# Flamingo layer on one core: each engine's repeated turn is replaced by one straight list over all eight batches

## The chip, the cores and the metric

One core of a Trainium2 chip runs the whole program. The metric is the device time of one execution in microseconds (us). The core has five engines that run side by side, each through its own instructions in order: TensorE (PE in the profile; PEld are its weight loads), VectorE (DVE), ScalarE (ACT), GpSimd (POOL) and SyncE (SP, which issues the DMAs). They wait for each other through semaphores.

## What is computed

For eight batches of 512 tokens with 256 features:

```python
emb  = layernorm(x) + ctx
q, k, v = emb @ wq + bq, emb @ wk + bk, emb @ wv + bv
ew   = exp(w - max(w));  w = pos_bias inside a band of 64, else 0
num  = ew @ (exp(k - max_k) * v);  den = ew @ exp(k - max_k)
attn = (sigmoid(q) * num / den) @ wo + bo
n1   = norm(attn + emb) * gamma + beta
n2   = norm(relu(n1 @ w1 + b1) @ w2 + b2 + n1) * gamma + beta
x1   = x + tanh(g_xattn) * n2
xq   = act_quant(layernorm(x1))
gate, up = silu(xq @ weight_quant(w_gate).T), xq @ weight_quant(w_up).T
out  = x1 + tanh(g_ffn) * (act_quant(gate * up) @ weight_quant(w_down).T)
```

`weight_quant` rounds a whole matrix to three values, by the mean of its magnitudes; `act_quant` rounds each token to 8 bits, by its maximum.

## The kernel before

A batch is four tiles of 128 tokens. Its work is cut into pieces, each a small function of one engine, named by batch `b` and a tile or half. In the order of the data they are:

- x and ctx come by `fetch_x`, `fetch_ctx` (SP, one buffer each). The first norm: `tile_stats(b, 0, t)` and `mean_variance` (DVE), `rsqrt(b, 0)` (POOL), `normalise(b, 0)` (ACT), `embed` (POOL) adds ctx. `emb_rows` transposes on PE; `emb_upper` (ACT) and `emb_lower` (DVE) split the result into a high and a low part, and this pair of splits follows every transposition of the float part: a product of two split operands is three matmuls (`product`, L1258 to L1267, so that all of them show as L1265).
- `keys_T`, then `key_max`, `max_bias` (DVE), `max_row` (PE) and `bias_parts` (DVE) give the row that `keys_values` (PE) adds to keys and values. `queries` and `half_sigmoid` (ACT) make the gate of attention. Per tile, `exp_keys`, `copy_values` (ACT), `weighted` (DVE), `e_upper` (ACT) and `e_lower` (DVE) make the pair e, ev.
- `attend(b, "num" or "den", half, j)` multiplies tile j's near weights; `key_sums`, `sum_upper`, `sum_lower` and `attend_far` add what lies outside the band. `inverse` (DVE reciprocal), `gated`, `divided`, `y_upper`, `y_lower`, `project` (PE), `first_residual` (DVE, on top of `add_bo` of POOL), norm 1 (`normalise_tile`), `n1_rows`, `n1_upper`, `n1_lower`.
- Feed-forward: eight of `hidden` (PE), `hidden_upper`, `hidden_whole` (ACT), `hidden_lower` (DVE), `feed_forward` (PE); `second_residual` (DVE), norm 2, `n2_gamma`, `first_sum` (POOL) give x1.
- The bit part: norm 3, `token_max`, `token_scales` (DVE), `token_quantise` (ACT), `xq_rows`, `xq_columns`; per tile `gate`, `up` (PE), `silu` (ACT), `product`, `product_scale` (DVE), `quantise` (POOL for even tiles, ACT for odd), `hq_rows` (PE), `hq_columns` (ACT), `down` (PE), `output` (DVE). `store` after four outputs.

Nearly all tiles in SBUF are single: x_in, emb, the pair e, n1T, a2, x1, out_t; h has four places. PSUM has eight banks for everything; `BANK_USES` gives each piece one bank (gate and up: two neighbours), the same for every batch, and `bank_wait` makes PE wait for the bank's last reader.

The order is written out: each engine has one function `turn(n, b0, ..., b4)`, with its pieces in a fixed order, where b2, b3, b4 are the batches n-2, n-3, n-4. `turns` calls it for n = 0 to 4 and 8 to 11 as straight code, and for n = 5, 6, 7 in a loop (`Fori`), in which the semaphore values are worked out from the loop's register. In a turn, b2 goes from the first norm to e and to `attend(b2, "num", 0 and 1, 0)`; b3 has the rest of attention, projection, norm 1, feed-forward, norms 2 and 3 up to `product(b3, 1)`; b4 has the rest of the bit part. The preparation of weights (`masks`, `position_max`, `exp_positions`, `positions_T`, `ewT_upper`; the splits; `sum_of_magnitudes`, `bit_scale`, `bit_round`, `bit_clip`, `bit_rows`, `bit_columns` for the three quantised matrices; `beta_w1` for b1) stands in the turns 0 to 3 under `if n == ...`.

## Time and profile before

| | us |
|---|---|
| median of 3 runs | 746.5 (746.36 to 746.93) |
| the profiled execution | 753.5 |
| its span, first to last instruction | 751.7 |
| busy in it: PE, DVE, ACT, POOL | 544.9, 439.7, 381.4, 213.7 |
| mean granted clock of TensorE, of full speed | 0.933 |
| moved between HBM and core | 25.12 MB |

The profile is of one execution. Its page lists busy times by engine, then the chain of work that ended last (followed back from the last instruction, at each step to what released it), then the costliest groups of instructions. Windows give each engine's busy time in a stretch; a timeline lists instructions by start. "x" is a count of instructions; L and a number is the line in the kernel, which can be that of a helper; in square brackets stands the idle time of an engine before an instruction, and what ended it. A clock of 1.00 is the higher of the two levels of TensorE (2.4 GHz), the lower is 1.2 GHz.

### The profile page before, as it was taken

The page shows a single profiled execution, that of the slowest core. Times are in us where ns is not written, and L with a number is a line of the kernel's source. Part 1 is how long each engine was busy: PE and PEld are TensorE (multiplying, and loading weights), DVE is VectorE, ACT ScalarE, POOL GpSimd, SP SyncE. Part 2 cuts the span into 40 slices and gives each one's busy share as a digit, 9 for nine tenths or more (in the row PEclk, how much of TensorE's full clock was granted, in tenths as well). Part 3 has the DMA queues.
Part 4 walks back from the last instruction along what each step waited for, and adds up shares of the span by engine and source line. Part 5 has one row for each costly group of instructions (what it writes and reads, how often), then busy time and mean ns, then how long its engine had stood idle before and what let it go on. Part 6 is the DMA issues. An engine that isn't in the chain of part 4 may idle for free.

```text
span 751.7 us, 10043 instructions
## 1 busy us (share of the span) xinstructions
PE 544.9 (72%) x3248; PEld 440.3 (59%) x3270; DVE 439.7 (58%) x907; ACT 381.4 (51%) x589; POOL 213.7 (28%) x232
## 2 busy tenths in 40 slices
PE   0539578587986779677968698777968697769534
PEld 0537567464865567555956486556846595547413
DVE  2254724568465954587366855596457836694236
ACT  0665145444646356644654565635664464545334
POOL 2330016301361026301640136102730155013211
PEclk9999879789998999899998999899989999899859
DMA  7540000200002000300030000200030001000000
GB/s 237 160 146 17 1 1 0 84 1 1 1 29 84 1 1 2 112 0 0 0 104 7 0 0 16 95 0 2 0 113 1 0 2 56 1 1 1 28 1 28
DMA packets 25208, 25.12 MB, mean 33 GB/s; under 512 B 3154, under 2 KB 24148, under 8 KB 25172
## 3 DMA queue, kind: packets, MB, share of 16 engines
q1 hardware_dynamic: 24336, 24.65, 10.0%
q8 instruction: 21, 0.34, 0.2%
q10 hardware_dynamic: 836, 0.01, 0.1%
q14 instruction: 15, 0.12, 0.1%
HBM read 20.46 MB, written 4.19 MB: 33 GB/s over the span
## 4 chain that ended last, share of the span: by engine, by line
PE 43%; DVE 29%; issue 10%; ACT 9%; POOL 4%; DMA 2%; SPq 1%; DVEq 0%; ACTq 0%; POOLq 0%
PE ps L1265 35%; DVE ps L976 5%; DVE st L920 4%; DVE cols L1049 2%; DVE work L1043 2%; POOL rstd L407 2%; DVE bias_row L953 2%; ACT work L587 2%; ACT work L593 2%; PE ps L1397 1%; ACT work L682 1%; DVE cols L1024 1%; DVE e_lo L967 1%; DVE work L1000 1%; DVE n1T_lo L1005 1%
## 5 line engine op out<-in xcount | busy, mean ns | idle before, releaser
L404 POOL TENSOR_TENSOR mv<-mv,cols 128x4 f32<-128x4 f32 x32 | 6.5, 204 | 326.2 <-DVE mv L928 326.2
L1011 DVE TENSOR_TENSOR h_lo<-ps,h_hi 128x512 fp32r<-128x512 f32 x64 | 43.5, 690 | 89.5 <-ACT ps L658 89.5
L653 ACT ACTIVATE h_hi<-ps,cols 128x512 fp32r<-128x512 f32 x64 | 44.1, 690 | 60.8 <-PE ps L1265 48.7
L682 ACT ACTIVATE work<-ps,cols 128x1024 f32<-128x1024 f32 x32 | 35.7, 1114 | 72.5 <-PE ps L1397 56.6
L1265 PE MATMUL ps<-w_hi,h_hi 128*128 128x256 f32 x256 | 72.2, 282 | 0.0
L1265 PE MATMUL ps<-w_lo,h_hi 128*128 128x256 f32 x256 | 72.1, 282 | 0.0
L1265 PE MATMUL ps<-w_hi,h_lo 128*128 128x256 f32 x256 | 71.9, 281 | 0.0
L1265 PE MATMUL ps<-ew_hi,e_hi 128*128 128x256 f32 x128 | 42.6, 333 | 37.5 <-DVE e_lo L967 37.5
L1043 DVE TENSOR_TENSOR work<-work,ps 128x1024 f32<-128x1024 f32 x32 | 38.8, 1213 | 41.6 <-ACT work L682 41.4
L1265 PE MATMUL ps<-n1T_hi,w_hi 128*128 128x512 f32 x128 | 52.2, 408 | 10.3 <-DVE n1T_lo L1005 10.3
L694 ACT ACTIVATE hqT<-ps,cols 128x1024 bf16<-128x1024 f16 x32 | 35.6, 1112 | 40.7 <-PE ps L1416 40.7
L976 DVE RECIPROCAL ps<-ps 128x512 f32<-128x512 f32 x16 | 53.8, 3359 | 0.8 <-PE ps L1342 0.6
L1424 PE MATMUL ps<-wdT,hqT 128*128 128x256 bf16 x256 | 33.2, 272 | 27.5 <-DVE work L1067 16.9
L1265 PEld LDWEIGHTS ps<-ew_hi,e_hi 128*128 128x128 f32 x128 | 28.7, 224 | 41.2 <-DVE e_lo L967 40.9
L1265 PE MATMUL ps<-n1T_lo,w_hi 128*128 128x512 f32 x128 | 51.4, 402 | 0.0
L1265 PE MATMUL ps<-n1T_hi,w_lo 128*128 128x512 f32 x128 | 51.2, 400 | 0.0
L1265 PEld LDWEIGHTS ps<-w_lo,h_hi 128*128 128x128 f32 x256 | 48.2, 188 | 1.4
L1265 PEld LDWEIGHTS ps<-w_hi,h_hi 128*128 128x128 f32 x256 | 48.0, 187 | 1.4
L1265 PEld LDWEIGHTS ps<-w_hi,h_lo 128*128 128x128 f32 x256 | 48.4, 189 | 0.0
L1424 PEld LDWEIGHTS ps<-wdT,hqT 128*128 128x128 bf16 x256 | 23.1, 97 | 36.2 <-issue 26.0
L587 ACT ACTIVATE work<-work,nmr,rstd 128x256 f32<-128x256 f32 x64 | 33.2, 589 | 21.8 <-POOL nmr L410 21.7
L1397 PE MATMUL ps<-wuT,xqT 128*128 128x512 bf16 x121 | 31.3, 391 | 14.0 <-DVE work L982 13.6
(180 smaller groups left out, 1561.4 us busy)
## 6 DMA issues: line engine op xcount, KB each, us to landing
x_in<-in_x_dram SPq DMA_DIRECT2D x8, 512.0 KB, 4.7
emb<-in_ctx_dram SPq DMA_DIRECT2D x8, 512.0 KB, 5.9
work<-in_x_dram SPq DMA_DIRECT2D x8, 512.0 KB, 3.7
out_dram<-work SPq DMA_DIRECT2D x8, 512.0 KB, 3.0
work<-in_L_xattn_w_dram SPq DMA_DIRECT2D x2, 1024.0 KB, 8.8
place_c<-in_L_xattn_pos_bias_dram SPq DMA_DIRECT2D x1, 1024.0 KB, 9.3
work<-in_L_ffn_w_gate_dram SPq DMA_DIRECT2D x1, 1024.0 KB, 5.5
work<-in_L_ffn_w_up_dram SPq DMA_DIRECT2D x1, 1024.0 KB, 5.7
```

The source lines that it names most:

```text
L407: pool.tensor_tensor(rstd[:, n, :], mv[:, n, :, 1], minus_half, ALU.pow).then_inc(rstd_ok[n].sem, 1)
L587: last = nc.scalar.activation(dst[:, t, :], src[:, t, :], ACT.Identity, bias=nmr[:, n, t:t + 1], scale=rstd[:, n, t:t + 1])
L653: nc.scalar.activation(h_hi[:, m % RING, :], bank("h", m), ACT.Relu, bias=b1_col[:, m:m + 1]).then_inc(h_hi_ok.sem, 1)
L682: nc.scalar.activation(sg, bank_pair("gate", t), ACT.Silu, scale=sgate[:, t:t + 1]).then_inc(sg_ok.sem, 1)
L694: nc.scalar.activation(hqT[:], bank_h("hqT", t).rearrange("p (k n) -> p k n", n=P), ACT.Identity, bias=unlift_col, scale=LIFT_SCALE).then_ ...
L920: nc.vector.bn_stats(st6[:, n, t, :], src[:, t, :]).then_inc(stats[n].sem, 1)
L976: nc.vector.reciprocal(bank("den", h), bank("den", h)).then_inc(rden_ok.sem, 1)
L1011: nc.vector.tensor_tensor(h_lo[:, m % RING, :], bank("h", m), h_hi[:, m % RING, :], ALU.subtract).then_inc(h_lo_ok.sem, 1)
L1043: nc.vector.tensor_tensor(prod[t % 2].rearrange("p (a n) -> p a n", a=2), sg.rearrange("p (a n) -> p a n", a=2), bank_pair("up", t), ALU.m ...
L1265: last = nc.tensor.matmul(dst, lhsT, rhs, start=(i == 0 and not begun), stop=(i == n - 1 and ends))
L1397: last = nc.tensor.matmul(dst[:, c, :], xqT[:, k, t * P:(t + 1) * P], w[:, k, c * T:(c + 1) * T], start=(k == 0), stop=(k == ND - 1))
L1424: last = nc.tensor.matmul(bank("down", t)[:, 0:D], hqT[:, k, :], wdT[:, k, :], start=(k == 0), stop=(k == NH - 1))
```

## The change

`turn`, `turns` and the loop are gone on all five engines. Each engine runs a straight list of pieces with constant batch numbers (536 on PE, 582 on DVE, 464 on ACT, 107 on POOL), in another order than the turns had. The pieces issue the same instructions as before. `BANK_USES` becomes `BANK`, with a bank for each piece and each batch; `bank_wait` follows the list and waits for the last reader of that bank; the banks used once for weights (`EWT_BANKS`, `TOTAL_BANKS`, `BIT_BANKS`, `B1_BANK`) are tracked the same way. On POOL some waits for vectors move from `rows` into the pieces that need them. The core of the diff:

```diff
-BANK_USES = (
-    ("xqT", 0, 4, 1, 1), ("gate", 0, 4, 0, 2), ("up", 0, 4, 6, 2), ("up", 1, 4, 2, 2), ("gate", 1, 4, 0, 2),
...
+BANK = {
+    ("embT", 0): (0, 5, 1, 5, 4, 0, 2, 6), ("embT", 1): (1, 4, 6, 7, 2, 6, 4, 0), ("kT", 0): (4, 4, 1, 0, 4, 0, 2, 6),
+    ("kT", 1): (5, 5, 6, 7, 0, 2, 6, 0), ("mx", 0): (0, 3, 1, 6, 1, 3, 7, 4), ("kv", 0): (0, 1, 7, 7, 4, 0, 2, 4),
+    ("kv", 1): (1, 3, 6, 6, 6, 4, 0, 0), ("kv", 2): (2, 6, 1, 2, 5, 1, 3, 1), ("kv", 3): (3, 4, 6, 3, 7, 5, 1, 2),
...
+    ("den", 1): (0, 2, 0, 1, 3, 7, 5, 5), ("o", 0): (0, 0, 7, 4, 0, 2, 1, 1), ("o", 1): (6, 6, 6, 5, 1, 3, 5, 2),
...
+    ("gate", 3): (0, 2, 6, 4, 4, 2, 6, 0), ("up", 3): (2, 6, 4, 0, 2, 6, 0, 4), ("hqT", 3): (7, 4, 0, 2, 5, 0, 4, 6),
...
+        held = {}
 
         def bank_wait(b, step, n=0):
...
+            first = BANK[step, n][b]
+            c, per = last_reader[step]
+            for place in range(first, first + (2 if step in PAIRED else 1)):
+                for s, k in held.get(place, ()):
+                    nc.tensor.wait_ge(s, k)
+                held[place] = ((c.sem, c.at(b, (n + 1) * per)),)
```

SP's list (`x_again` is the second load of x, for x1):

```diff
-                if b2 is not None:
-                    fetch_x_again(b2)
-                if n == 2:
-                    fetch_gate()
-
-            turns(sp, turn)
+            fetch_positions()
+            fetch_w2()
+            fetch_x_again(0)
+            fetch_ctx(0)
+            fetch_x(0)
+            fetch_wqo()
+            fetch_gate()
+            fetch_w1()
+            fetch_x(1)
+            fetch_wkv()
+            fetch_vectors()
+            fetch_ctx(1)
+            fetch_up()
+            fetch_down()
+            fetch_x(2)
+            fetch_ctx(2)
+            fetch_x(3)
+            fetch_x_again(1)
+            fetch_ctx(3)
+            fetch_x(4)
+            store(0)
+            fetch_x_again(2)
+            fetch_ctx(4)
+            fetch_x(5)
+            store(1)
+            fetch_x_again(3)
+            fetch_ctx(5)
+            fetch_x(6)
+            store(2)
+            fetch_x_again(4)
+            fetch_ctx(6)
+            fetch_x(7)
+            store(3)
+            fetch_x_again(5)
+            fetch_ctx(7)
+            store(4)
+            fetch_x_again(6)
+            store(5)
+            fetch_x_again(7)
+            store(6)
...
```

PE's list: its head, one cycle of the steady part, and the end.

```diff
+            positions_T()
+            emb_rows(0, 0)
+            emb_rows(0, 1)
+            total(0)
+            queries(0, 0)
+            queries(0, 1)
+            bit_rows(0)
+            keys_T(0, 0)
+            keys_T(0, 1)
+            max_row(0)
+            beta_w1()
+            keys_values(0, 0)
+            keys_values(0, 1)
+            keys_values(0, 2)
+            keys_values(0, 3)
+            attend(0, "num", 0, 0)
+            attend(0, "den", 1, 0)
+            attend(0, "den", 1, 1)
+            attend(0, "den", 0, 0)
+            attend(0, "den", 0, 1)
+            emb_rows(1, 0)
...
+            project(3, 0)
+            project(3, 1)
+            project(3, 2)
+            project(3, 3)
+            keys_values(4, 0)
+            keys_values(4, 1)
+            keys_values(4, 2)
+            keys_values(4, 3)
+            hq_rows(1, 3)
+            attend(4, "num", 0, 0)
+            attend(4, "den", 1, 0)
+            attend(4, "den", 1, 1)
+            attend(4, "den", 0, 0)
+            attend(4, "den", 0, 1)
+            down(1, 3)
+            attend(4, "den", 1, 2)
+            attend(4, "den", 0, 2)
+            attend(4, "num", 1, 0)
+            attend(4, "num", 0, 1)
+            key_sums(4)
+            n1_rows(3, 0)
+            attend(4, "den", 1, 3)
+            n1_rows(3, 1)
+            attend(4, "num", 0, 2)
+            attend(4, "num", 0, 3)
+            attend_far(4, "num", 0)
+            attend(4, "den", 0, 3)
+            attend_far(4, "den", 0)
+            attend_far(4, "den", 1)
+            attend(4, "num", 1, 1)
+            hidden(3, 0)
+            attend(4, "num", 1, 2)
+            attend(4, "num", 1, 3)
+            attend_far(4, "num", 1)
+            hidden(3, 1)
+            hidden(3, 2)
+            feed_forward(3, 0)
+            feed_forward(3, 1)
+            xq_rows(2)
+            hidden(3, 3)
+            hidden(3, 4)
+            hidden(3, 5)
+            hidden(3, 6)
+            feed_forward(3, 2)
+            gate(2, 0)
+            up(2, 0)
+            emb_rows(5, 0)
+            feed_forward(3, 3)
+            feed_forward(3, 4)
+            gate(2, 1)
+            gate(2, 2)
+            hidden(3, 7)
+            up(2, 1)
+            hq_rows(2, 0)
+            feed_forward(3, 5)
+            up(2, 2)
+            down(2, 0)
+            up(2, 3)
+            emb_rows(5, 1)
+            feed_forward(3, 6)
+            keys_T(5, 0)
+            keys_T(5, 1)
+            hq_rows(2, 1)
+            feed_forward(3, 7)
+            hq_rows(2, 2)
+            down(2, 1)
+            queries(5, 0)
+            down(2, 2)
+            max_row(5)
+            queries(5, 1)
+            gate(2, 3)
+            project(4, 0)
+            project(4, 1)
+            project(4, 2)
+            project(4, 3)
+            keys_values(5, 0)
+            keys_values(5, 1)
+            keys_values(5, 2)
+            keys_values(5, 3)
...
+            feed_forward(7, 6)
+            xq_rows(6)
+            feed_forward(7, 7)
+            gate(6, 0)
+            up(6, 0)
+            gate(6, 1)
+            gate(6, 2)
+            up(6, 1)
+            up(6, 2)
+            up(6, 3)
+            hq_rows(6, 0)
+            gate(6, 3)
+            down(6, 0)
+            hq_rows(6, 1)
+            down(6, 1)
+            hq_rows(6, 2)
+            down(6, 2)
+            hq_rows(6, 3)
+            down(6, 3)
+            xq_rows(7)
+            gate(7, 0)
...
```

DVE's list over a part of the head, and a part of a cycle:

```diff
+            emb_lower(0, 0)
+            emb_lower(0, 1)
+            bit_scale(0)
+            tile_stats(1, 0, 0)
+            tile_stats(1, 0, 1)
+            tile_stats(1, 0, 2)
+            bit_clip(0)
+            tile_stats(1, 0, 3)
+            mean_variance(1, 0)
+            wkv_lower()
+            key_max(0, 0)
+            key_max(0, 1)
+            max_bias(0)
+            bias_parts(0)
+            b1_whole()
+            w1_lower()
+            weighted(0, 0)
...
+            tile_stats(2, 0, 2)
+            tile_stats(2, 0, 3)
+            bit_clip(1)
+            gated(0, 0)
+            bit_clip(2)
+            gated(0, 1)
+            inverse(0, 0)
+            weighted(1, 0)
+            divided(0, 0)
+            inverse(0, 1)
...
+            bias_parts(4)
+            first_residual(3, 0)
+            tile_stats(3, 1, 0)
+            tile_stats(3, 1, 1)
+            product(1, 3)
+            first_residual(3, 1)
+            product_scale(1, 3)
+            weighted(4, 0)
+            tile_stats(3, 1, 2)
+            tile_stats(3, 1, 3)
+            weighted(4, 1)
+            mean_variance(3, 1)
+            e_lower(4, 0)
+            weighted(4, 2)
+            e_lower(4, 1)
+            e_lower(4, 2)
+            weighted(4, 3)
+            output(1, 3)
+            e_lower(4, 3)
+            tile_stats(2, 3, 0)
+            tile_stats(2, 3, 1)
+            tile_stats(2, 3, 2)
+            tile_stats(2, 3, 3)
+            sum_lower(4)
+            mean_variance(2, 3)
+            n1_lower(3, 0)
+            n1_lower(3, 1)
+            inverse(4, 0)
...
```

POOL's list over one cycle, and the start of ACT's:

```diff
+            rsqrt(3, 1)
+            first_sum(2)
+            n1_gamma(3)
+            rsqrt(2, 3)
+            add_b2(3)
+            x_beta(3)
+            add_bo(4)
+            embed(5)
+            quantise(2, 0)
+            rsqrt(6, 0)
+            quantise(2, 2)
...
+            w2_upper()
+            exp_positions()
+            ewT_upper(0)
+            ewT_upper(1)
+            ewT_upper(2)
+            ewT_upper(3)
+            wo_upper()
+            wq_upper()
+            normalise(0, 0)
+            sum_of_magnitudes(0)
+            emb_upper(0, 0)
+            emb_upper(0, 1)
+            bit_round(0)
+            wkv_upper()
+            bit_columns(0)
+            normalise(1, 0)
+            w1_upper()
+            gates_and_bias()
+            half_sigmoid(0, 0)
+            half_sigmoid(0, 1)
+            exp_keys(0, 0)
...
```

## Rows read from the trace of the kernel before

**Rows 1.** The page: busy time, ended-last chain by engine, three groups (busy, mean ns | idle before)
```profile
PE 544.9 (72%) x3248; PEld 440.3 (59%) x3270; DVE 439.7 (58%) x907; ACT 381.4 (51%) x589; POOL 213.7 (28%) x232
...
PE 43%; DVE 29%; issue 10%; ACT 9%; POOL 4%; DMA 2%; SPq 1%; DVEq 0%; ACTq 0%; POOLq 0%
...
L1011 DVE TENSOR_TENSOR h_lo<-ps,h_hi 128x512 fp32r<-128x512 f32 x64 | 43.5, 690 | 89.5 <-ACT ps L658 89.5
...
L1043 DVE TENSOR_TENSOR work<-work,ps 128x1024 f32<-128x1024 f32 x32 | 38.8, 1213 | 41.6 <-ACT work L682 41.4
...
L976 DVE RECIPROCAL ps<-ps 128x512 f32<-128x512 f32 x16 | 53.8, 3359 | 0.8 <-PE ps L1342 0.6
```

**Rows 2.** Windows: start:end, length, busy PE, PEld, DVE, ACT, POOL, clock, DMA share, GB/s
```profile
52.00:100.42 48.42, 34.65 (x181) 29.22 (x181) 25.91 (x44) 20.39 (x32) 3.72 (x5) 0.87 0.07 23
270.34:352.37 82.03, 64.27 (x394) 51.80 (x397) 52.41 (x109) 44.38 (x70) 25.21 (x27) 0.96 0.08 26
352.37:434.20 81.83, 64.34 (x393) 51.83 (x397) 52.39 (x109) 44.36 (x70) 25.15 (x27) 0.96 0.08 26
598.58:680.05 81.47, 63.97 (x393) 51.67 (x397) 52.25 (x108) 44.53 (x70) 28.68 (x29) 0.96 0.04 14
703.00:751.70 48.70, 18.14 (x127) 10.33 (x126) 21.52 (x55) 19.46 (x24) 10.28 (x14) 0.77 0.06 22
```

**Rows 3.** Windows inside one turn, columns as above
```profile
352.37:375.30 22.93, 22.93 (x146) 20.77 (x147) 8.89 (x22) 13.83 (x22) 11.34 (x9) 1.00 0.00 0
392.30:397.60 5.30, 0.03 (x1) 0.00 (x0) 3.05 (x8) 5.05 (x11) 0.00 (x0) 0.78 0.47 154
397.60:413.00 15.40, 14.96 (x82) 11.87 (x85) 9.83 (x17) 6.32 (x8) 1.29 (x2) 0.86 0.00 0
```

**Rows 4.** The chain that ended last, inside the same turn: start, length, what
```profile
382.84 2.22 DVE bias_row L953
...
394.48 1.23 DVE cols L1024
```

**Rows 5.** Timeline of PE: start, length, instruction; at the low and the high clock
```profile
398.20 0.41 PE L1265 MATMUL ps<-ew_hi,e_lo 128*128 128x256 f32 x1
398.41 0.41 PE L1265 MATMUL ps<-ew_hi,e_hi 128*128 128x256 f32 x1
...
439.56 0.28 PE L1265 MATMUL ps<-w_hi,h_hi 128*128 128x256 f32 x1
439.67 0.28 PE L1265 MATMUL ps<-w_lo,h_hi 128*128 128x256 f32 x1
...
439.91 0.39 PE L1265 MATMUL ps<-n1T_hi,w_hi 128*128 128x512 f32 x1
440.14 0.39 PE L1265 MATMUL ps<-n1T_lo,w_hi 128*128 128x512 f32 x1
```

**Rows 6.** Timeline of the head, all engines: start, length, instruction, idle before
```profile
9.51 0.28 DVE L831 CAST bias_row<-bkv_row 1x256 fp32r<-1x256 f32 x1 [6.75 <-DMA bkv_row<-in_L_xattn_bv_dram]
...
12.21 1.93 POOL L378 TENSOR_SCALAR_AFFINE_SELECT place_c<-place_c 128x2048 f32<-128x2048 f32 x1 [10.64 <-DMA place_c<-in_L_xattn_pos_bias_dram]
...
20.83 1.91 ACT L540 ACTIVATE w_hi<-work 128x2048 fp32r<-128x2048 f32 x1 [15.80 <-DMA work<-in_L_xattn_w_dram]
...
28.77 6.83 PE L1237 MATMUL ps<-cols,work 128*128 128x1 f32 x32
...
51.91 1.94 PE L1273 MATMUL ps<-ident,emb 128*128 128x128 f32 x8
...
61.33 0.47 PE L1310 MATMUL ps<-bias_row,ones_r 128*128 128x512 f32 x1
```

**Rows 7.** Timeline of the tail, columns as above
```profile
712.53 2.34 POOL L449 TENSOR_TENSOR work<-work 128x1024 f32<-128x1024 f32 x1
...
726.99 0.14 PEld L1397 LDWEIGHTS ps<-wgT,xqT 128*128 128x128 bf16 x2 [1.64 <-issue]
...
747.87 0.48 DVE L1067 SCALAR_TENSOR_TENSOR work<-ps,cols,work 128x256 f32<-128x256 f32 x1 [2.47 <-PE ps L1424]
```

2162 lines of the change are left out of this document (1607 added, 555 removed), and 5 rows, old and new, of the table BANK.

## The prediction

> **What bounds the kernel now.** I read the page first. The matrix engine (PE) is the busiest at 544.9 us, yet that is 72% of the span, and the chain that ended last is only 43% PE [rows 1]: no engine is full, so order and latency set the time. The windows cut at each batch's first `hidden` matmul show the rhythm: every batch costs 81.5 to 82.0 us, of which PE is busy 64, DVE 52, ACT 44, POOL 25 to 29 [rows 2]. The windows inside one turn show where PE's missing 17.5 us are. In the feed-forward stretch PE is full (22.93 of 22.93); behind keys_values it stands still for 5.3 us, and then runs a stretch at a mean granted clock of 0.86, part of it at 1.2 GHz [rows 3]. The chain says why: behind keys_values of batch b2 the third norm of b3 is worked off (ACT normalises, DVE takes the token maximum at 394.48), and only then comes e_lower(b2, 0), for which `attend` waits [rows 4]; later two reciprocals of 3.36 [rows 1] and the first norm stand between attention and feed-forward of the same batch. So one turn is 22.93 us of feed-forward plus a 59 us chain in which PE has 41.4 us of work. A turn holds attention, projection, norm and feed-forward of **one** batch (b3), which makes that chain unavoidable in it.
>
> **The change, part by part.**
>
> *No loop.* Nine of twelve turns were written out before; three (n = 5 to 7) ran in the loop. The batches whose period lies within the loop took 82.0 and 81.8 us, and one wholly written out 81.5 [rows 2]. So writing out is worth 0 to 0.5 us for each of three turns; I take 0. The Trainium skill (Runtime: NRT & Kernel Launch, Instruction fetch mechanics) says that a taken branch breaks the sequential prefetch and forces a stall, while a long straight program streams; by it something would be gained per pass. By those rows it is under 0.5 us, and I add nothing.
>
> *PSUM banks per batch, semaphores on constants.* No added instruction; each bank waits for its last reader only. Price 0, above zero only where a chosen bank ties two stages: in the list for batch 4, `o` of batch 3 lies in banks 4 and 5, which kv 0 and kv 2 of batch 4 take, and `up(…, 3)` in banks 6 and 7, which kv 1 and kv 3 take. These readers stand just before in DVE's list; I count 1.5 us of PE idleness per cycle for them.
>
> *The new order.* In the steady part, between two feed-forwards of batch f, PE now has project(f+1), keys_values(f+2), nearly all of attend(f+2), key_sums(f+2) and n1_rows(f+1). The first norm of f+1 runs under kv and attend of f+2; reciprocals of f+2 run under hidden(f); gate, up and down of f-1 are spread through the feed-forward of f. What follows what across the waits:
> - PE's own work. Two 512-column matmuls start 0.23 us apart, two 256-column ones at the high clock 0.12, as 48 of the one and 96 of the other make 22.93 us; at the low clock 0.21 [rows 3, 5]. Counted out by these, a batch is 61 us; the 64.3 of [rows 2] less the excess of the 15 attend matmuls and 8 transposes run slowly (about 2 us) gives 62. I take 62.
> - Entry to kv: bias_parts must be done. Its cast took 2.22 us [rows 4] where the same cast elsewhere took 0.28 [rows 6]; with the rest it is 1.2 to 3.1 us after max_row, and PE has queries(…, 1), gate(…, 3) and four projects, 5.2 us, in between. Covered at either price. The Trainium skill (SBUF — State Buffer, SBUF: two separate sides) has a reason: a cast in a two-port mode and a GpSimd instruction lock each other out; POOL has no large operation at that place of the new lists. By the rule the cast falls back to 0.28, by the old row it stays; the sum is the same.
> - kv to attend: DVE has ahead of e_lower(…, 0) two residual additions (0.69 each, as h_lo), product(…, 3) (1.21 [rows 1]), its maximum (1.23, as the token maximum [rows 4]) and some fifteen instructions of 0.1 to 0.45: about 8 us, against 7.2 us of kv and hq_rows on PE plus the bank waits above; then e_lower(…, 3) about 5 us later against 4.1 us of attends. Idle: 1 + 1 us.
> - Feed-forward stretch: with gate, up and down in it, PE has 35 us of work and DVE about 33 busy (two reciprocals of 3.36 [rows 1], eight h_lo, three products with maxima), 35 with its gaps. They are level, so I allow 1 us.
> - POOL: the sums end about 2 us before emb_rows needs them. Free, with little cover; if they come late, all of the lateness is paid in each cycle.
>
> Together 62 + 4.5 = **66.5 us per batch** where it was 81.9.
>
> *The head.* Before, positions landed as about the second MB (masks at 12.2), w2 as the fifth (20.8), and emb_rows(0) began at 51.9 [rows 6]: some 0.24 MB/us. Now positions are first, then w2, x and ctx of batch 0: they land at about 7, 11 and 16.5. Masks to 11, maximum, w2_upper, exponentials to 16, transposes and ewT to 21, two weight copies, normalise(0, 0) to 24, embed to 26.5: emb_rows(0) at 27. But SP holds wkv behind fetch_x(1), which waits for that embed: wkv lands at 33; keys_T(0) at 34.5; then beta_w1 (6.8 us, [rows 6]) waits for the vectors, which are queued behind wkv, and keys_values(0) starts near 45, where it was 61.3 [rows 6]. w_up waits for beta_w1 and w1_lower, w_down behind it lands near 58; its rounding and clips stand in ACT's and DVE's lists ahead of batch 0's division. So the last attend_far(0) comes at 66, project(0) at 80, and hidden(0, 0) at **93** (100.4 before), but with attention of batch 1 already done.
>
> *Between.* hidden(0) to hidden(1) has no gate work and no cover for batch 1's norms: 24 us of feed-forward, 9.5 to kv(2), 15 of kv, attend and n1: **49**. Then five cycles at 66.5 (1 to 6): **332.5**. From hidden(6) to hidden(7) there is no new batch: 43 us of PE work and some idleness: **47**. Feed-forward of 7: **24**.
>
> *The tail.* Before, 48.7 us follow the last feed-forward [rows 2]; gate and down of batch 6 were long under way. The new list leaves all of gate(6) to down(6) behind feed_forward(7, 7), and first_sum(7) waits for the fourth output of 6. One batch from its first gate weights to its last output took 726.99 to 748.35, so 21.4 us; from first_sum to the end of the span it was 712.53 to 751.7, so 39.2 [rows 7]. With batch 7's second norm mixed in: 21.4 + 39.2 + 1.4 = **62**, 13 us more than now.
>
> *Sum.* 93 + 49 + 332.5 + 47 + 24 + 62 = 607.5 us of span. The profiled execution took 753.5 us (span 751.7, 1.8 around it), 7.0 above the median of 746.5; so 607.5 + 1.8 - 7.0 = **602.3 us**.
>
> **The rivals.**
> - *DVE becomes the bound.* For: 52.4 us busy [rows 2], an in-order list of 109 instructions, level with PE in the longest stretch. Against: 14 us of slack per cycle. It decides where DVE's waits per cycle exceed those; at 20 us of waits the period is 73: 5 x 6.5 = 32 more, 635.
> - *PE is filled.* For: the waits that I counted are each about 1 us and the cast is cheaper. Period 62.5: 20 less, 582.
> - *The chain stays.* The change doesn't do what it says: single buffers (x_in, emb, e, n1T, a2, x1) or a bank tie batch f+1 to f as before and the period stays 82: 602 + 5 x 15.5 = 680. Against: the longest ring that I find, output(f) to store to ctx to embed to quantise(f+1) to output(f+1), is some 40 us.
> - *Slower: SP's queue as a convoy.* store(b) stands before x_again(b+2) and ctx(b+3); if every load waits out the whole bit part of an old batch, stages run in series. To reach 746 the period must be (751.7 - 275) / 5 = 95 us, so the ring of 40 would need to be over twice as long. It is not in the rows.
>
> **How the numbers follow.** Forecast (590 to 620) 0.58; DVE-bound (620 to 650) 0.20; PE filled (575 to 590) 0.13; chain stays (650 to 744) 0.07; slower 0.02. The range 580 to 640 leaves out the two last and the outer ends of the second and third. A measurement of this kernel tells 0.2% (1.5 us) from no change; within that lies nearly nothing: 0.01. Faster 0.97, slower 0.02.
>
> **What would show it.** In the profile after: hidden of neighbouring batches 66.5 us apart in the middle and PE busy about 62 of it at a granted clock near 1.0; no gap of 5 us before the first attend; the cast of bias_parts at 0.3 us; emb_rows(0) near 27, hidden(0, 0) near 93; 62 us after the last feed-forward. I am wrong if the gaps before e_lower or product(…, 0) are several us, if beta_w1 or w_down come late, or if the head's waits push hidden(0, 0) past 100.

## The result and the profile after

The changed kernel takes **591.4 us** (median of 4 runs, 589.24 to 592.88); the kernel before took 746.7 us beside it. The ratio is 0.790 (95% interval 0.786 to 0.795). The forecast was 602.3 us, range 580 to 640: the direction is right, the time lies inside the range, and the forecast was 10.9 us too high.

The profiled execution took 589.24 us, its span 587.5. Its page, with the lines that answer to [rows 1] (busy time, share, instructions; then groups with busy time, mean ns | idle before them and its releaser):

```profile
PE 509.9 (87%) x3270; PEld 416.9 (71%) x3270; DVE 438.4 (75%) x907; ACT 373.3 (64%) x587; POOL 216.5 (37%) x232
...
L1436 DVE TENSOR_TENSOR h_lo<-ps,h_hi 128x512 fp32r<-128x512 f32 x64 | 42.9, 680 | 19.2 <-ACT ps L741 19.1
...
L1401 DVE RECIPROCAL ps<-ps 128x512 f32<-128x512 f32 x16 | 53.7, 3354 | 1.2 <-PE ps L2220 1.2
L1468 DVE TENSOR_TENSOR work<-work,ps 128x1024 f32<-128x1024 f32 x32 | 38.7, 1211 | 20.6 <-ACT work L765 17.6
```

The work is nearly the same: DVE was busy for 438.4 us (before 439.7), and a reciprocal still takes 3354 ns. ACT loads its table 12 times instead of 14, 1.3 us each. What went is idleness: DVE stood 19.2 us in front of h_lo where it had stood 89.5, and PE is busy 87% of the span instead of 72%.

The windows of after, cut as in [rows 2] at each batch's first `hidden` matmul (start:end, length, then busy PE, PEld, DVE, ACT, POOL, granted clock, DMA share, GB/s): the head, hidden(0) to hidden(1), 1 to 2, two steady cycles, and what follows the last feed-forward:

```profile
0.00:98.72 98.72, 62.83 (x366) 54.22 (x367) 64.99 (x128) 54.71 (x86) 32.38 (x38) 0.90 0.37 112
98.72:141.48 42.76, 42.52 (x262) 37.49 (x263) 31.91 (x72) 24.92 (x48) 19.45 (x21) 1.00 0.12 38
141.48:208.43 66.95, 64.74 (x421) 53.34 (x420) 54.03 (x111) 44.25 (x71) 25.66 (x28) 1.00 0.10 32
208.43:271.07 62.64, 61.04 (x397) 50.05 (x397) 51.85 (x109) 43.72 (x70) 25.35 (x27) 1.00 0.11 35
271.07:333.70 62.63, 61.03 (x397) 50.04 (x397) 51.84 (x109) 43.72 (x70) 25.40 (x27) 1.00 0.11 35
...
525.00:587.50 62.50, 31.57 (x200) 16.95 (x198) 34.25 (x81) 29.11 (x33) 12.86 (x18) 0.78 0.05 18
```

A batch costs 62.64 us instead of 81.9. Of these 19.3 us, 16.0 are PE idleness (17.6 before, 1.6 now) and 3.3 are PE's own busy time (64.3 to 61.03): the granted clock of a cycle rose from 0.96 [rows 2] to 1.00, and the stretch at 0.86 behind the gap of 5.3 us [rows 3] is gone with the gap.

| stretch | forecast | measured | difference |
|---|---|---|---|
| start to hidden(0, 0) | 93 | 98.7 | +5.7 |
| hidden 0 to 1 | 49 | 42.8 | -6.2 |
| hidden 1 to 6, five cycles | 332.5 | 314.6 | -17.9 |
| hidden 6 to 7 | 47 | 45.3 | -1.7 |
| feed-forward of 7 | 24 | 23.6 | -0.4 |
| from there to the end | 62 | 62.5 | +0.5 |
| span | 607.5 | 587.5 | -20.0 |
| from span to median | -5.2 | +3.9 | +9.1 |
| median | 602.3 | 591.4 | -10.9 |

Where PE stood in the kernel before, over three cycles (270.34 to 515.85 us; line, releaser: us in total, times, longest):

```profile
PE ps L1265 <- DVE e_lo L967: 15.9, 3, 5.4
PE ps L1424 <- DVE work L1067: 7.4, 3, 2.5
PE ps L1397 <- DVE work L982: 5.8, 3, 1.9
PE ps L1265 <- DVE n1T_lo L1005: 5.1, 4, 1.3
PE ps L1265 <- DVE work L982: 4.2, 3, 1.4
...
PE ps L1359 <- ACT work L593: 0.3, 2, 0.2
```

The idleness was spread over about a dozen places. The largest is the 5.3 us in front of `attend`, which waits for `e_lower`. In front of `n1_rows` (L1359), where the first norm must be done, PE stood only 0.2 us: `up`, `down` and `hq_rows` of the older batch lay ahead of it, with 2.5 us of waiting in front of that `down` (L1424). 1.3 us more followed in front of `hidden` (n1T_lo). The 1.4 us in front of `queries` and the 1.9 us in front of `up` are waits for a bank: PE waits until `gated` (L982) has read the bank that it is to write.

Two things said ahead of the result were wrong. The pieces don't all issue the same instructions as before: in `bias_parts` the diff turns `nc.vector.tensor_copy(bias_row[0:1, 0:D], mrow)` into `nc.vector.tensor_tensor(bias_row[0:1, 0:D], mrow, mrow, ALU.max)`, one instruction per batch, which I had overlooked. And the lists have 576 pieces on PE, 586 on DVE and 468 on ACT, where 536, 582 and 464 were given.

### The profile page after: what moved, and what is told of

The parts are those of the page before. It is cut to its first block and busy times, and to the rows that moved or that the text cites. A ratio compares the mean times of both kernels' runs of the same rounds, so it can differ in the third digit from the quotient of the medians.

```text
span 587.5 us, 9784 instructions
## 1 busy us (share of the span) xinstructions
PE 509.9 (87%) x3270; PEld 416.9 (71%) x3270; DVE 438.4 (75%) x907; ACT 373.3 (64%) x587; POOL 216.5 (37%) x232
## 5 line engine op out<-in xcount | busy, mean ns | idle before, releaser
L2143 PE MATMUL ps<-w_hi,h_hi 128*128 128x256 f32 x256 | 75.2, 294 | 5.3 <-DVE h_lo L1436 5.3
L1436 DVE TENSOR_TENSOR h_lo<-ps,h_hi 128x512 fp32r<-128x512 f32 x64 | 42.9, 680 | 19.2 <-ACT ps L741 19.1
L1401 DVE RECIPROCAL ps<-ps 128x512 f32<-128x512 f32 x16 | 53.7, 3354 | 1.2 <-PE ps L2220 1.2
L1468 DVE TENSOR_TENSOR work<-work,ps 128x1024 f32<-128x1024 f32 x32 | 38.7, 1211 | 20.6 <-ACT work L765 17.6
L461 POOL TENSOR_TENSOR cols<-cols 1x1 f32<-1x1 f32 x16 | 2.9, 183 | 130.8 <-DVE cols L1483 130.7
L1345 DVE BATCH_NORM_STATS2 st<-work 128x6 f32<-128x256 f32 x96 | 34.9, 413 | 12.0 <-POOL work L456 11.5
L741 ACT ACTIVATE ps<-ps,cols 128x512 f32<-128x512 f32 x64 | 41.7, 652 | 0.0
L1474 DVE TENSOR_REDUCE cols<-work 128x1 f32<-128x1024 f32 x32 | 38.8, 1211 | 0.4
```

Of the source, the lines that this page charges most:

```text
L741: nc.scalar.activation(bank(b, "h", m), bank(b, "h", m), ACT.Relu, bias=b1_col[:, m:m + 1]).then_inc(h_relu_ok.sem, 1)
L1345: nc.vector.bn_stats(st6[:, n, t, :], src[:, t, :]).then_inc(stats[n].sem, 1)
L1401: nc.vector.reciprocal(bank(b, "den", h), bank(b, "den", h)).then_inc(rden_ok.sem, 1)
L1436: nc.vector.tensor_tensor(h_lo[:, m % RING, :], bank(b, "h", m), h_hi[:, m % RING, :], ALU.subtract).then_inc(h_lo_ok.sem, 1)
L1468: nc.vector.tensor_tensor(prod[t % 2].rearrange("p (a n) -> p a n", a=2), sg.rearrange("p (a n) -> p a n", a=2), bank_pair(b, "up", t), AL ...
L1474: nc.vector.tensor_reduce(hm[:, t:t + 1], prod[t % 2], AX.X, ALU.max, apply_absolute_value=True).then_inc(hm_ok.sem, 1)
```

## The experiments

Medians of device time; ratios are to the kernel before, timed on the same chip, with 95% intervals. Periods are the distances between neighbouring hidden(b, 0) in the profiled execution.

### Is it the loop?

This is the kernel before with its three looped turns written out:

```diff
-            for n in range(TURNS):
-                whole(n)
-            with eng.Fori(TURNS, NB) as n:
-                turn(None, *[n - age for age in range(TURNS)])
-            for n in range(NB, NB + TURNS - 1):
+            for n in range(NB + TURNS - 1):
                 whole(n)
```

> The kernel before with its loop written out: the same turns in the same order, twelve times straight code, all waits on constants. Theory (the order brought the gain, the loop cost nothing): 746.5 us, within 1.5 of it, since batches inside and outside the loop had the same period (82.0, 81.8 and 81.5 us). Rival (giving up the loop is itself worth something: branches, semaphore values from registers): up to 0.5 us per turn by the rows, more if a stall hides elsewhere: 740 or less.

Measured: 747.23 us (10 runs), ratio 1.0015 [0.9976, 1.0053]. The batches whose period lies in the former loop take 81.4 to 82.4 us, as the others. Giving up the loop was worth nothing that can be measured, so the gain is that of order and banks together; no run separates these two. The Trainium skill (Runtime: NRT & Kernel Launch, Instruction fetch mechanics) says that a taken branch whose target has not been fetched stalls the engine; over these three turns no such stall shows.

### What is the changed instruction worth?

The instruction was changed once alone in the kernel before, and once undone in the changed kernel:

```diff
-                nc.vector.tensor_copy(bias_row[0:1, 0:D], mrow).then_inc(bias_hi_ok.sem, 1)
+                nc.vector.tensor_tensor(bias_row[0:1, 0:D], mrow, mrow, ALU.max).then_inc(bias_hi_ok.sem, 1)
```

> The kernel before with one instruction changed, the one that the diff also changed in bias_parts: tensor_copy(bias_row, mrow) becomes tensor_tensor(mrow, mrow, max). In the turns the copy takes 2.2 us and lies on the chain that ended last; it ends just as POOL's n2_gamma ends. If only the copy's mode makes it wait for POOL, the new form takes 0.4 us there too and each of seven turns is up to 1.8 us shorter: 746.5 - 12 = 734 us. If an instruction with two inputs in SBUF waits for POOL as well (as the Trainium skill says, SBUF — State Buffer, SBUF: two separate sides), nothing changes: 746.5 us, and the 0.41 us of the kernel after come from POOL standing idle at that place of its list.

> The kernel after with the old tensor_copy put back in bias_parts, everything else as it is. Theory (bias_parts is covered by queries, gate and four projects on PE in the new order): 591.4 us, within 2, whether the copy takes 0.3 or 2.3 us. Rival (the replaced copy was a real part of the gain): 1.9 us for each of seven batches, 604 us.

Measured: 748.18 us, ratio 1.0025 [0.9991, 1.0058], and 594.25 us, ratio 0.796 [0.791, 0.801]. The instruction itself, by line (duration ns min/median/max; first and last start), in the kernel before, in before with the maximum, in the changed kernel and in that with the copy:

```profile
L953 DVE CAST bias_row<-bkv_row x8: 280/2206/2222, 60.5 to 628.9; 1x256 fp32r<-1x256 f32 x8
```

```profile
L953 DVE TENSOR_TENSOR bias_row<-bkv_row x8: 413/2345/2351, 58.8 to 622.1; 1x256 fp32r<-1x256 f32 x8
```

```profile
L1378 DVE TENSOR_TENSOR bias_row<-bkv_row x8: 411/411/414, 45.4 to 439.9; 1x256 fp32r<-1x256 f32 x8
```

```profile
L1378 DVE CAST bias_row<-bkv_row x8: 280/282/282, 45.6 to 443.1; 1x256 fp32r<-1x256 f32 x8
```

In the old place both forms take over 2.2 us (medians); in the new one they take 0.28 and 0.41. The place decides, not the form; my theory of a gain in the old kernel fell. In the lists the copy gives periods of 62.66, so it is covered, as the prediction had it. The medians of the two lists differ by 2.8 us, and by 1.7 us against the changed kernel run again (592.53, below). In the profiled executions the kernel with the copy was 1.5 us longer between hidden(1) and hidden(2) and 1.6 us longer after the last feed-forward than the changed kernel. In the first of these stretches PE's waits are the same and the granted clock is 0.98 against 1.00, and the instruction itself is shorter (0.28 against 0.41); so nothing points at the instruction.

### Is it the cover of the first norm?

The kernel is the changed one, but for batches 3 to 5 `n1_rows(b, ·)` stands right behind `project(b, 3)` on PE, ahead of kv and attend of batch b+1; on ACT and DVE the pieces that feed it are moved forward with it. The core of the diff, for b = 3:

```diff
             normalise_tile(3, 0)
...
+            n1_lower(3, 0)
+            n1_lower(3, 1)
...
+            n1_rows(3, 0)
+            n1_rows(3, 1)
...
-            n1_rows(3, 0)
...
-            n1_rows(3, 1)
```

> The kernel after, where for batches 3, 4 and 5 the first norm is no longer covered: on PE n1_rows(b) stands right behind project(b, 3) and before keys_values(b+1), and DVE's and ACT's parts of that norm are moved ahead of the e parts of b+1 to match. Same instructions, same PE work. Theory (the gain is the cover of such chains by the next batch's work): residual, statistics, rsqrt, four normalise and n1_rows show on PE as 7 to 9 us of idleness in each of three cycles: 591.4 + 24 = 615 us. Rival (the gain is a better filling in general, and other work closes such a gap): under 3 us per cycle, below 600 us.

Measured: 626.22 us, ratio 0.839 [0.833, 0.844]; the three periods are 71.6, 73.8 and 75.0 us: 9.0, 11.1 and 12.4 more. What PE waited for in 208 to 435 us (line, releaser: us in total, times, longest), and one of these cycles in the columns of the windows:

```profile
PE ps L2237 <- ACT work L676: 21.7, 3, 7.4
PE ps L2143 <- DVE h_lo L1436: 4.9, 3, 1.8
```

```profile
283.85:357.62 73.77, 63.45 (x395) 52.36 (x397) 52.98 (x109) 44.03 (x70) 25.30 (x28) 0.93 0.09 30
```

PE stands 7.2 us in front of n1_rows, the granted clock of the cycle is 0.93, and PE's busy time is 63.45 instead of 61.03. This shows that in the new order the norm needs the cover, which is worth 9 to 12 us per batch. It does not show that this cover brought the gain. In the kernel before, n1_rows was not uncovered in this way: work of the older batch lay between the projection and it, and PE stood 2.5 us in front of the `down` ahead of it, 0.2 us in front of it and 1.3 us in front of `hidden`, 4.0 us together. Its largest wait, 5.3 us for `e_lower` behind the third norm of the batch ahead, was not put back alone by any run, nor were its waits for banks. How the 19.3 us divide is therefore open.

### What sets 62.64 us: PE, DVE, or neither?

Four runs on the changed kernel. In the first, PE is relieved: the third product of `feed_forward` is left out, so the output lacks that product. In the second, DVE is loaded with a reduction that nobody needs. In the third, DVE is relieved: h_lo has one column instead of 512 and h_hi takes its place in the product, so the output lacks the low part of h. In the fourth, both are relieved.

```diff
-                    last = product(bank(b, "f", t // 2)[:, t % 2 * D:(t % 2 + 1) * D],
-                                   [(h_hi[:, m % RING, c], h_lo[:, m % RING, c], w2_hi[:, m, :], w2_lo[:, m, :])],
-                                   begun=(m > 0 or t % 2 > 0), ends=(m == NH - 1 and t % 2 == 1))
+                    dst = bank(b, "f", t // 2)[:, t % 2 * D:(t % 2 + 1) * D]
+                    for i, w in enumerate((w2_hi, w2_lo)):
+                        last = nc.tensor.matmul(dst, h_hi[:, m % RING, c], w[:, m, :],
+                                                start=(m == 0 and t % 2 == 0 and i == 0),
+                                                stop=(m == NH - 1 and t % 2 == 1 and i == 1))
```

> The kernel after with less PE work and nothing else: feed_forward leaves out its third product (low part of h by high part of w2), 32 matmuls of 0.12 us per batch, 3.84 us; h_lo is still computed. The output is that of a less exact product. Theory (PE is the bound from the first to the last feed-forward): the time falls by nearly all of it in every batch, 8 x 3.84 = 31 us, to 561 us; the steady period from 62.65 to 58.8. Rival (DVE's list or the waits bound the steady cycle): less than half arrives, 576 us or more, and PE's idle time per cycle grows from 1.6 to 4 us.

```diff
+                nc.vector.tensor_reduce(waited, h_lo[:, 0:2, :].bitcast(F32), AX.XY, ALU.max)
```

> The kernel after with one more DVE reduction of 128x1024 (1.21 us) behind each product_scale, 4.85 us of DVE work per batch that nobody waits for. Theory (PE is the bound, DVE has 10.8 us of room per cycle of 62.65): steady period up by 0 to 1.5 us, and up to 8 us in the tail, where batches 6 and 7 run through DVE alone: 596 to 605 us. Rival (DVE is level with PE): all of it counts, 5 x 4.85 in the middle and 8 in the tail: 624 us.

```diff
-                nc.vector.tensor_tensor(h_lo[:, m % RING, :], bank(b, "h", m), h_hi[:, m % RING, :],
+                nc.vector.tensor_tensor(h_lo[:, m % RING, 0:1], bank(b, "h", m)[:, 0:1], h_hi[:, m % RING, 0:1],
...
-                                   [(h_hi[:, m % RING, c], h_lo[:, m % RING, c], w2_hi[:, m, :], w2_lo[:, m, :])],
+                                   [(h_hi[:, m % RING, c], h_hi[:, m % RING, c], w2_hi[:, m, :], w2_lo[:, m, :])],
```

> The kernel after with less DVE work: hidden_lower subtracts one column instead of 512 (8 x 0.53 = 4.2 us less per batch), and feed_forward's third product takes h_hi where h_lo was, so PE's work stays. The low part of h is left out of the output. Theory, formed on the last runs (DVE's list rules the steady cycle, PE stands 1.2 us behind): the period falls from 62.65 to about PE's own 61.0 to 61.4, 591 - 8 = 583 us with the ends. Rival (PE alone rules, and the DVE work that was added cost by its place only): no change of the period, 590 us or more.

The fourth has the short h_lo and the left-out product together.

> Both kinds of work less: the third product of feed_forward left out (3.84 us of PE per batch) and hidden_lower on one column (4.2 us of DVE). Theory (both lists are level, each hides the other's gain): the period falls by far more than the 1.2 us that PE's alone gave, to about 58.5 to 59.5 us; 565 us. Rival (a chain through ACT and POOL rules, neither of the two): the period stays above 61 us, 580 us or more.

One steady cycle of each, in the order of the table, in the columns of the windows:

```profile
332.86:394.37 61.51, 58.05 (x364) 46.10 (x365) 51.64 (x109) 43.84 (x70) 25.36 (x27) 1.00 0.11 35
```

```profile
279.72:346.13 66.41, 61.54 (x396) 50.01 (x397) 55.93 (x113) 43.88 (x70) 25.34 (x27) 1.00 0.10 33
```

```profile
274.00:336.10 62.10, 61.06 (x397) 50.03 (x397) 48.56 (x109) 43.66 (x70) 25.38 (x27) 1.00 0.11 35
```

```profile
331.04:391.90 60.86, 58.00 (x364) 46.07 (x365) 48.41 (x109) 43.72 (x70) 25.36 (x27) 1.00 0.12 36
```

| run | PE busy | DVE busy | period | change | median, us | ratio |
|---|---|---|---|---|---|---|
| changed kernel | 61.03 | 51.84 | 62.64 | | 591.42 | 0.790 |
| PE relieved | 58.05 | 51.64 | 61.50 | -1.14 | 587.59 | 0.789 [0.786, 0.791] |
| DVE loaded | 61.54 | 55.93 | 66.41 | +3.77 | 623.00 | 0.837 [0.834, 0.840] |
| DVE relieved | 61.06 | 48.56 | 62.10 | -0.54 | 590.00 | 0.790 [0.784, 0.795] |
| both relieved | 58.00 | 48.41 | 60.86 | -1.78 | 579.69 | 0.776 [0.771, 0.782] |

My theory that PE is the bound fell: with 3.0 us less of busy time the period falls by 1.14 and PE's idleness grows from 1.6 to 3.5 us. "DVE is the bound" falls with the third run: 3.3 us less of DVE work gives 0.54. Yet 4.1 us more at the products costs 3.8, although DVE had 10.8 us of idleness per cycle. The two reliefs about add up (1.14 + 0.54 = 1.68, measured 1.78). With the load, PE gets three new waits in each cycle (213 to 412 us, three cycles):

```profile
PE ps L2295 <- DVE cols L1365: 5.1, 3, 1.7
...
PE ps L2276 <- DVE work L1468: 2.6, 3, 0.9
PE ps L2295 <- DVE e_lo L1392: 2.2, 3, 0.7
```

All three are waits for a bank: `hq_rows` waits until `key_max` or `e_lower` has read the bank that it is to write (its own data, from POOL's or ACT's `quantise`, was there 1.2 and 2.2 us earlier), and `up` waits for `product`. So late work on DVE reaches PE here through the bank map. Whether another map would have carried less of it was not tried. That what is taken away at one place is waited off at the next fits the two reliefs; it is a reading, not an experiment.

For one place the trace shows what happens. This is PE's only large gap in the cycle of the changed kernel, by the timeline (start, length, instruction, idle before), with DVE and POOL around it:

```profile
279.21 0.38 PE L2143 MATMUL ps<-w_hi,h_hi 128*128 128x256 f32 x1 [1.32 <-DVE h_lo L1436]
```

```profile
275.18 0.67 DVE L1436 TENSOR_TENSOR h_lo<-ps,h_hi 128x512 fp32r<-128x512 f32 x1
275.77 0.33 DVE L1454 TENSOR_SCALAR cols<-cols 128x4 f32<-128x4 f32 x1
276.13 0.18 DVE L1457 RECIPROCAL cols<-cols 128x4 f32<-128x4 f32 x1
276.23 2.21 DVE L1459 TENSOR_SCALAR cols<-cols 128x4 f32<-128x4 f32 x1
278.35 0.22 DVE L1461 TENSOR_SCALAR cols<-cols 128x4 f32<-128x4 f32 x1
278.48 0.68 DVE L1436 TENSOR_TENSOR h_lo<-ps,h_hi 128x512 fp32r<-128x512 f32 x1
```

```profile
273.66 2.42 POOL L431 TENSOR_TENSOR work<-work,tbeta_all 128x1024 f32<-128x1024 f32 x1
276.02 2.39 POOL L425 TENSOR_TENSOR work<-emb,bo_all 128x1024 f32<-128x1024 f32 x1
```

L1459 scales 128x4 numbers, works from SBUF to SBUF and takes 2.21 us; L1461, the same on the same tile, takes 0.22. L1459 ends at 278.44 with POOL's addition (276.02 + 2.39 = 278.41), and h_lo(1), for which PE stands still, comes right behind L1461 on DVE. In the kernel before its like (L1034) took 0.20 us in all eight batches. The run with the short h_lo agrees with this reading:

```profile
278.95 2.38 POOL L425 TENSOR_TENSOR work<-emb,bo_all 128x1024 f32<-128x1024 f32 x1
```

```profile
279.15 2.21 DVE L1459 TENSOR_SCALAR cols<-cols 128x4 f32<-128x4 f32 x1
281.27 0.22 DVE L1461 TENSOR_SCALAR cols<-cols 128x4 f32<-128x4 f32 x1
281.41 0.14 DVE L1436 TENSOR_TENSOR h_lo<-ps,h_hi 128x1 fp32r<-128x1 f32 x1
```

```profile
281.60 0.38 PE L2143 MATMUL ps<-w_hi,h_hi 128*128 128x256 f32 x1 [0.79 <-DVE h_lo L1436]
```

L1459 still ends with POOL; h_lo(1) is 0.54 us shorter, PE's gap behind it 0.53 (1.32 to 0.79), and the period 0.54. All eight h_lo of a batch had been shortened, and the period fell by no more than this one gives. With less work on PE ahead of it the gap grows to 1.8 us, which is where part of that relief went. To issue L1459 behind h_lo(1) was not tried, so the hold by POOL is read from the ends that agree, and what the next wait would leave of the 1.3 us is open.

### The tail

For batch 7 the last sum and the output go into `x_in` and `emb`, which nobody needs any more, so that `first_sum(7)` needn't wait for the outputs of batch 6; then, in a second step, the pieces of batch 7 are put ahead of the outputs of 6:

```diff
-                wait(pool, out_ok, b, 0)
-                pool.tensor_tensor(x1, n2, xb, ALU.add).then_inc(x1_ok.sem, 1)
+                if b < NB - 1:
+                    wait(pool, out_ok, b, 0)
+                pool.tensor_tensor(x1_of(b), n2, xb, ALU.add).then_inc(x1_ok.sem, 1)
```

> The kernel after; batch 7 alone keeps x1 in the tile x_in and its normalised x and output in the tile emb, both free by then, so that first_sum(7) need not wait for the fourth output of batch 6 nor normalise(7, 3) for its store. Lists unchanged. Theory (in the tail the order stands in the way as much as the buffer): first_sum(7) moves from 547.4 to about 538.6, but tile_stats(7, 3) stays behind output(6, 3) at 547.2 in DVE's list: 2.6 us gained, 589 us. Rival (the buffer alone held it): 9 us or more gained, 582 us.

```diff
+            first_sum(7)
...
-            first_sum(7)
...
+            normalise(7, 3)
...
-            normalise(7, 3)
...
-            output(6, 0)
-            product_scale(6, 3)
-            output(6, 1)
-            output(6, 2)
-            output(6, 3)
...
+            output(6, 0)
+            product_scale(6, 3)
+            output(6, 1)
+            output(6, 2)
...
+            output(6, 3)
```

> As the one before, and first_sum(7), tile_stats(7, 3), mean_variance(7, 3), normalise(7, 3), token_max(7) and token_scales(7) are moved ahead of the last pieces of batch 6 in POOL's, DVE's and ACT's lists. Theory (the two bit parts of the tail stand one behind the other because of x1 and of the order): the third norm of 7 runs beside tiles 2 and 3 of batch 6, xq_columns(7) ends near 551 instead of 561.7: 11 us gained, 580 us. Rival (the tail is bound by DVE and ACT work of two batches): under 4 us, 588 us.

Measured: 588.67 us, ratio 0.792 [0.788, 0.795], and 583.88 us, ratio 0.784 [0.781, 0.786]. From the last feed-forward to the end it is 62.5, about 59.4 and about 53.3 us. The last sum of batch 7 on POOL, in the changed kernel and in the second step:

```profile
547.41 2.34 POOL L456 TENSOR_TENSOR work<-work 128x1024 f32<-128x1024 f32 x1 [8.86 <-DVE work L1492]
```

```profile
536.78 2.36 POOL L467 TENSOR_TENSOR x_in<-work 128x1024 f32<-128x1024 f32 x1
```

In the first, POOL stands 8.86 us for an output of batch 6, and the sum starts 22.7 us behind the first gate matmul after the last feed-forward (524.72); in the second it starts 10.7 us behind it (526.12). In the tail, tiles alone gave 3.1 us, tiles and order together 9.2 of the 13.8 us by which the new lists had made it longer. The order without the tiles was not run, and what the other 4.6 us are was not found. The medians fell by less than the tail, 2.8 and 7.5 us; the head differs between executions too (hidden(0, 0) at 100.4 and 100.2 us in the two profiles, 98.7 in that of the changed kernel; see below).

### The head, on top of it

```diff
-    ("embT", 0): (0, 5, 1, 5, 4, 0, 2, 6), ("embT", 1): (1, 4, 6, 7, 2, 6, 4, 0), ("kT", 0): (4, 4, 1, 0, 4, 0, 2, 6),
+    ("embT", 0): (6, 5, 1, 5, 4, 0, 2, 6), ("embT", 1): (7, 4, 6, 7, 2, 6, 4, 0), ("kT", 0): (4, 4, 1, 0, 4, 0, 2, 6),
...
+                nc.scalar.activation(nwmax, wmax, ACT.Copy, scale=-1.0).then_inc(nwmax_ok, 1)
...
-                nc.vector.tensor_scalar(nwmax, wmax, -1.0, None, ALU.mult).then_inc(nwmax_ok, 1)
...
-                nc.vector.tensor_copy(far_w[:], far_f[:]).then_inc(far_hi_ok, 1)
+                nc.vector.tensor_reduce(far_w[:], far_f[:].rearrange("p (n a) -> p n a", a=1), AX.X, ALU.max).then_inc(far_hi_ok, 1)
```

Besides, `fetch_x_again(0)` stands behind the fetch of wqo, and `fetch_down` ahead of the context of batch 1.

> The kernel of the tail's new order with four edits in the head: the negated maximum is made by ACT, far_w by a reduction over one element instead of a copy (both had been held up 1.5 to 2.4 us on DVE while POOL ran w2_lower and embed(0)), emb_rows(0) writes banks 6 and 7 that do not wait for far_w, and SP fetches the second x of batch 0 later and w_down before ctx of batch 1. Theory (a DVE instruction in a two-port mode waits for POOL, a reduction does not): exp_positions starts at 15.2 instead of 17.6, emb_rows(0) at 28 instead of 31.4, hidden(0, 0) 3 us earlier: 584 - 3 = 581 us. Rival (those waits are covered by loads): no gain, 584 us.

> The kernel after, unchanged, on the same chip and in the same rounds as the three others, to measure their differences against it: 589 to 593 us as before. If it lies at 593 to 595, the 2.8 us that the kernel with the old copy seemed to cost are the chip's and the clock's, not the copy's.

Measured: **577.59 us**, ratio 0.773 [0.769, 0.777], the fastest of all; the changed kernel again 592.53, ratio 0.793 [0.789, 0.797]. hidden(0, 0) comes at 94.5 us. Two stretches of the head in the changed kernel (POOL's line is from the timeline of the same execution), then the same place in the new one:

```profile
13.05 4.50 POOL L397 TENSOR_TENSOR w_lo<-work,w_hi 128x2048 fp32r<-128x2048 f32 x1 [1.30 <-ACT w_hi L623]
...
27.92 2.35 POOL L417 TENSOR_TENSOR emb<-x_in,emb 128x1024 f32<-128x1024 f32 x1 [3.58 <-ACT x_in L670]
```

```profile
15.00 2.58 DVE L1288 TENSOR_SCALAR cols<-cols 128x4 f32<-128x4 f32 x1
...
28.59 1.96 DVE L1305 CAST far_w<-far_f 128x512 fp32r<-128x512 f32 x1
30.59 0.68 DVE L1307 TENSOR_TENSOR far_w<-far_f,far_w 32x512 fp32r<-32x512 f32 x1
```

```profile
25.68 2.36 POOL L427 TENSOR_TENSOR emb<-x_in,emb 128x1024 f32<-128x1024 f32 x1 [3.65 <-ACT x_in L686]
```

```profile
26.35 0.69 DVE L1319 TENSOR_REDUCE far_w<-far_f 128x512 fp32r<-128x512 f32 x1
27.07 1.50 DVE L1321 TENSOR_TENSOR far_w<-far_f,far_w 32x512 fp32r<-32x512 f32 x1
```

In the changed kernel the negation of 128x4 numbers (L1288), for which the exponentials wait, takes 2.58 us and ends with POOL's 4.5 us instruction; the cast of far_w takes 1.96 and ends at 30.55, with POOL's addition running from 27.92 to 30.27. The same copy written as a reduction over one element takes 0.69 in the midst of POOL's addition; the subtraction behind it, which has two inputs in SBUF, is the one that is now held: it takes 1.50 instead of 0.68. On PE the transposes of the first batch:

```profile
31.41 1.94 PE L2151 MATMUL ps<-ident,emb 128*128 128x128 f32 x8 [7.52 <-DVE far_w L1307]
```

```profile
28.09 1.97 PE L2165 MATMUL ps<-ident,emb 128*128 128x128 f32 x8 [6.44 <-POOL emb L427]
```

They start 3.3 us earlier and wait for their data, no more for the banks that far_w was read from. The edits were made together, so the 6.3 us below the run without them aren't divided among them. The head varies from execution to execution: hidden(0, 0) came at 98.7 us in the first profile of the changed kernel and at 102.5 in its second, with the same periods. The two traces show where: `beta_w1` took 4.27 us in the first and 6.42 in the second, and from 80 to 98.7 us the granted clock was 1.00 in the first and 0.82 in the second.

```profile
44.78 4.27 PE L2113 MATMUL ps<-cols,work 128*128 128x1 f32 x32
```

```profile
44.89 6.42 PE L2113 MATMUL ps<-cols,work 128*128 128x1 f32 x32
```

The kernel with the four edits had the short `beta_w1` (4.24 us), so the first profile is the one to compare it with: keys_values(0) starts at 44.7 us instead of 48.9, and hidden(0, 0) comes at 94.5 instead of 98.7. By these profiles the edits are worth 4.2 us; the rest of the 6.3 may be the clock's.

## Why the prediction was right, and where not

- **What bounds the kernel before.** Right in the main: order and latency, not a full engine. PE's idleness per cycle fell from 17.6 to 1.6 us, and neither the loop nor the changed instruction has a part in it. The 5.3 us behind the third norm were read rightly. The first norm was given too much weight: PE stood 4.0 us in all from the `down` ahead of n1_rows to hidden, and 7.2 us came only when the run on the new order left it without any cover. Left out were the waits for banks: 1.4 us in front of `queries`, 1.9 us in front of `up`, and the last 1.2 of the 2.5 us in front of `down` (`output` ends at 430.0 us, the other input of `down` at 428.9).
- **No loop.** Priced 0; measured 1.0015 [0.9976, 1.0053]. Right.
- **Banks per batch.** Priced 1.5 us of each cycle. Wrong by all of it: PE's idleness in a cycle is 1.6 us in total, and its two waits (1.32 for h_lo, 0.25 for n1T_lo) are for data. That the change of banks could also gain something was priced at 0, though the kernel before had the waits for banks named above; how much the new map took of them, apart from the order, no run shows. In the cycle the ties cost only under more DVE work (3.3 us with the loaded DVE). The one tie that cost something as it stands was in the head, where I had not looked: emb_rows(0) stood for far_w until 31.41, 1.1 us behind the end of its own data's addition (30.27).
- **PE's own work, 62.** Measured 61.03. I had counted 61 from the spacings at the high clock, and then taken 62, from the measured 64.3 less about 2 us for the work that ran at the low clock. With the gap gone the clock is 1.00 in the whole cycle; the count from spacings was the right one. 1.0 us per cycle.
- **kv to attend, 1 + 1.** Measured no gap on PE at either place. I had set DVE's queue (8 us, added up from single durations) against PE's time (7.2) and taken a difference of 0.8 and its like for idleness; the sums are not good to that. 2 us per cycle.
- **Feed-forward stretch, 1.** Measured 1.3, for another reason than the level lists that I named: the held L1459.
- Together the period was set **3.9 us** too long: banks 1.5, kv to attend 2, PE's work 1.0, less 0.6 because the idleness that did come was 1.6 where the feed-forward term had 1.0. Over the five cycles, of which the first and last are not steady (66.9 and 59.7), this makes 17.9 us. The steady period is the term of the sum that was mis-sized most.
- **The cast.** "Covered at either price": right. The reason given agrees with the rows: without a large POOL instruction at that place it takes 0.28. But I applied the rule to the one instruction whose row I had seen, and asked for no other instruction that the new order would put under a POOL addition. There are three that matter: L1288 and L1305 in the head, and L1459 in every steady cycle (0.2 us in the kernel before). The Trainium skill (SBUF — State Buffer, SBUF: two separate sides) names the two kinds: DVE instructions in a two-port mode, and those with two inputs in SBUF against a GpSimd instruction that reads it; whichever starts first holds the ports for its whole length. The rows here agree: each of the three starts after POOL's instruction and ends with it or shortly behind (0.03 us for the 2.58 and the 2.21, 0.28 us for the 1.96), and the maximum of two SBUF inputs took 2.35 where the copy took 2.2.
- **POOL, 2 us of cover.** PE never waits for it in a steady cycle; its lateness shows only on DVE (2.08 us in front of the statistics). What it does to DVE's instructions was the part left out.
- **The head, 93.** Measured 98.7. Forecast emb_rows(0) at 27, it came at 31.4: up to 2.4 us for the held negation, about 1.1 for the banks, the rest in single waits. keys_values(0) began at 48.9 instead of 45, although beta_w1 took 4.27 us instead of 6.8 in this execution (6.42 in another); 1.8 us more arose between there and hidden(0, 0).
- **hidden 0 to 1, 49.** Measured 42.76 with PE busy 42.52. I had added the idleness of an uncovered stretch where there was enough work of batch 1 in front.
- **The tail, 62.** Measured 62.5, by the forecast's own steps: gate to down of batch 6 behind the last feed-forward, 22.7 us (forecast 21.4 + 1.4), then from first_sum(7) to the end 40.1 us (39.2). The experiment on it shows that 9.2 us of the tail could be had back with two tiles and an order.
- **From span to median.** I subtracted the 7.0 us by which the profiled execution of before lay above its median. That belonged to that execution: the changed kernel's profile lay 2.2 below its median. Without the subtraction the forecast would have been 609.3, 17.9 too high. So the 10.9 us are in part luck: the period and the stretch from hidden 0 to 1 were set too long by 24.1 us, the head too short by 5.7, and the step from span to median was off by 9.1 the other way.
- **The rivals.** "PE is filled" gave a period of 62.5 and 582 us: its period came (62.64), and the median lies in the forecast's own class (590 to 620) by 1.4 us only. Its reason came in part: PE is busy 97% of the cycle, but taking 3.0 us of its work away brings 1.1. "DVE becomes the bound" did not come either, though the extra load shows that at the products DVE has almost no slack (3.8 us paid of 4.1). The busy shares, PE 97% of the cycle and DVE 83%, did not tell this. "The chain stays" and the slower one didn't come.

## What to carry to other kernels

When a pipeline of in-order engines has a long chain of one batch in each turn, list the waits of the busiest engine over one cycle, those for data and those for a buffer's last reader, and put another batch's work where they stand; count PE's work from start spacings at the high clock when the gaps are to go, since here the clock came back with them. After every reordering, look in the new timeline for small DVE instructions of 2 us: those looked at here ended with a POOL instruction, and one matters if the matrix engine's next input stands behind it. When a run takes the new order back at one place, check that the old kernel stood that way before calling the difference a part of the gain. And keep the start and the end of a straight list apart from its middle: an order that is right in steady state made the tail 14 us longer, 9 of which came back by two free tiles and a few moved lines.
